# Layer-1 score masks and the guards' schedule moved towards VectorE's queue in a two-layer graph-attention kernel

## The reference

```
adj  = maximum(adj, eye(n))
keys, queries, values = x @ Wks, x @ Wqs, x @ Wvs          # per head
atts = einsum('hqk,hmk->hqm', queries, keys) / key_dim**0.5
atts = atts - 1e16 * (1.0 - adj)
atts = softmax(atts, axis=-1)
out  = einsum('hqm,hmk,hko->qo', atts, values, Wo)
```

## Time and profile before

| what | us |
|---|---|
| median of 3 runs (4674.9 to 4680.1) | 4676.87 |
| the profiled execution, its own time | 4677.4 |
| its span, first to last instruction | 4675.6 |
| TensorE busy, share of the span | 4440.1, 95% |
| VectorE busy | 3542.8, 76% |
| GpSimd busy | 3434.2, 73% |
| ScalarE busy | 3246.9, 69% |
| TensorE granted clock, mean of the span | 0.978 of full speed |

### The profile page before, as it was taken

The page is one execution under the profiler, slowest core; times in us unless marked ns, Lnnn a source line. Parts: engine busy times, 40 slices in busy tenths (PEclk is TensorE's granted clock), DMA queues, the critical chain, the costliest instruction groups (busy, mean ns, idle before and its releaser), DMA issues. The chain is left out here.

```text
span 4675.6 us, 112897 instructions
## 1 busy us (share of the span) xinstructions
PE 4440.1 (95%) x43276; PEld 2137.3 (46%) x43276; DVE 3542.8 (76%) x7470; ACT 3246.9 (69%) x6022; POOL 3434.2 (73%) x2955
## 2 busy tenths in 40 slices
PE   8699999999999978969999999999999999999998
PEld 4222222222222224416556655656655566556555
DVE  5498998988989843367777777777777777777776
ACT  5366666666666633318878878878878788788786
POOL 2476676676776720029989989989989899899897
PEclk9899999999999989969999999999999999999999
DMA  3566776676676533353333433433423334334333
GB/s 143 131 210 196 202 224 201 204 211 208 206 213 184 169 112 112 106 174 86 111 112 92 127 101 90 127 101 99 124 83 111 112 93 130 98 88 127 103 102 102
DMA packets 462941, 646.14 MB, mean 138 GB/s; under 512 B 49536, under 2 KB 271104, under 8 KB 452288
## 3 DMA queue, kind: packets, MB, share of 16 engines
q1 hardware_dynamic: 383968, 522.36, 37.7%
q10 hardware_dynamic: 73856, 100.83, 6.8%
q0 software_dynamic: 4576, 15.73, 1.2%
HBM read 528.38 MB, written 110.38 MB: 137 GB/s over the span
## 5 line engine op out<-in xcount | busy, mean ns | idle before, releaser
L1398 POOL TENSOR_TENSOR d_PL<-d_PF,d_PH 128x512 f16<-128x512 f32 x2048 | 2324.3, 1171 | 296.0 <-ACT d_PH L1448 293.1
L1488 DVE CUSTOM_DVE_ANT_0 d_junk<-d_gd,d_MR 128x512 bf16<-128x512 f32 x2112 | 1441.9, 689 | 500.4 <-issue 465.3
L1444 ACT ACTIVATE d_PF<-d_sc 128x512 f32<-128x512 f32 x2048 | 1283.1, 627 | 518.4 <-DVE d_sc L1577 317.2
L1448 ACT ACTIVATE d_PH<-d_sc 128x512 f16<-128x512 f32 x2048 | 1292.3, 631 | 0.0
L809 DVE SCALAR_TENSOR_TENSOR b_P<-R,u,b_A 128x512 f32<-128x512 f32 x1792 | 1195.3, 738 | 108.8 <-PE b_den L867 58.8
L860 PE MATMUL b_acc<-b_P,V 128*64 128x512 f32 x4096 | 967.7, 608 | 77.8 <-DVE b_P L809 38.3
L1616 PE MATMUL d_gd<-d_KA,d_QA 128*128 128x512 f16 x2112 | 815.6, 387 | 60.6 <-DMA d_KA<-scratch_kl 30.6
L1632 PE MATMUL d_sc<-d_QA,d_KA 128*128 128x512 f16 x2048 | 776.8, 379 | 2.1 <-DVE d_QL L1501 2.1
L1633 PE MATMUL d_sc<-d_QL,d_KB 128*128 128x512 f16 x2048 | 776.3, 379 | 0.0
L1653 PE MATMUL d_acc<-d_V,d_PH 128*128 128x65 f16 x8192 | 638.9, 192 | 2.9 <-ACT d_PH L1448 0.2
L1655 PE MATMUL d_acc<-d_V,d_PH 128*128 128x64 f16 x8192 | 639.9, 193 | 0.0
(11 more groups left out here) (133 smaller groups left out, 4352.7 us busy)
## 6 DMA issues: line engine op xcount, KB each, us to landing
d_V<-scratch_v SPq DMA_DIRECT2D x131, 520.0 KB, 4.6
stage<-in_adjT SPq DMA_DIRECT2D x128, 512.0 KB, 4.5
b_srow<-in_adj ACTq DMA_DIRECT2D x256, 256.0 KB, 5.0
b_rows<-in_adj SPq DMA_DIRECT2D x112, 512.0 KB, 6.6
d_MR<-scratch_mr SPq DMA_DIRECT2D x36, 1024.0 KB, 5.4
d_MT<-scratch_mt SPq DMA_DIRECT2D x35, 1024.0 KB, 6.3
d_KA<-scratch_kh SPq DMA_DIRECT2D x272, 128.0 KB, 3.0
d_KA<-scratch_kl SPq DMA_DIRECT2D x272, 128.0 KB, 3.2
```

The lines of the kernel that those rows point to most:

```text
L1398: eng.tensor_tensor(PL[:, t % H_RING, :], PF[:, t % F_RING, :], PH[:, t % H_RING, :], ALU.subtract).then_inc(s_lowp if by_pool(t) else s_l ...
L1444: nc.scalar.activation(PF[:, t % F_RING, :], sc[(nb * TILES + t) % BANKS][:, :], ACT.Exp, scale=EXP_SCALE)
L1448: nc.scalar.activation(PH[:, t % H_RING, :], sc[(nb * TILES + t) % BANKS][:, :], ACT.Exp, scale=EXP_SCALE).then_inc(s_P, 1)
L1488: nc.vector.tensor_tensor_reduce(out=junk[:, gi % 2, :], in0=gd[gi % 2][:, :], in1=MR[:, s, c * QB:(c + 1) * QB], scale=1.0, scalar=-3.0e3 ...
```

## The change

Three things, all in `layer1_attention`:

1. `masked_by_vector`: before, every fourth tile (`t % 4 == 3`: x = 1 of the odd steps; 64 a block). After, in pair 0 every second tile (x = 1 of every step), in the other pairs `t % 8` in 3, 5, 7 (x = 1 of every step but 0, 4, 8, ..., 28). That is 32 + 3 * 24 = 104 a block. For each tile that changes sides, the matmul L1635 goes and an instruction L1577 comes; ScalarE then waits for VectorE.
2. `guards_of`: still 64 a pair, now from step 1 to step 28, three in the steps 4, 8, 12, 14, 16, 20, 24 and 28, two in the others. ROW_FREE moves from steps 9, 16, 23, 29 to 9, 15, 22, 29 of pair 2.
3. `mask_setup` moves from step 6 of pair 2 to its step 29, and the four `mask_diagonal` from `ROW_FREE + 4` (steps 13, 20 and 27 of pair 2 and step 1 of pair 3) to steps 30 and 31 of pair 2 and 0 and 3 of pair 3.

```diff
-    FIRST_G, LAST_G = 2, 28
+    FIRST_G, LAST_G, EXTRA_G = 1, 28, 14
...
+    def guard_count(mb):
+        if not FIRST_G <= mb <= LAST_G:
+            return 0
+        return 3 if mb % 4 == 0 or mb == EXTRA_G else 2
+
     def guards_of(mb):
-        def upto(step):
-            return GUARDS * min(max(step - FIRST_G + 1, 0), LAST_G - FIRST_G + 1) // (LAST_G - FIRST_G + 1)
-        return range(upto(mb - 1), upto(mb))
+        first = sum(guard_count(k) for k in range(mb))
+        return range(first, first + guard_count(mb))
+
+    assert sum(guard_count(mb) for mb in range(NT)) == GUARDS
...
-    DIAG_STEP, SETUP_STEP = (HP - 2) * NT + 1, (HP - 2) * NT + 6
-    ROW_SET = [free + 4 for free in ROW_FREE]
+    DIAG_STEP, SETUP_STEP = (HP - 2) * NT + 1, (HP - 1) * NT - 3
+    ROW_SET = [(HP - 1) * NT + late for late in (-2, -1, 0, 3)]
...
     def masked_by_vector(t):
-        return t % 4 == 3
+        return t % 2 == 1 if t < PAIR else t % 8 in (3, 5, 7)
```

## The result

The changed kernel takes 4604.16 us (median of 4 runs, 4600.57 to 4608.29) against 4678.42 for the kernel before in the same runs: ratio 0.9845, 95% interval 0.9833 to 0.9857, 74 us faster. I had forecast 4655 with a range of 4610 to 4688: right in sign, wrong in size, outside the range by 6 us. The time lies close to the first rival, "TensorE stays the bound throughout" (4593), but not by that rival's sum alone: the experiments show that more than a third of the gain comes from the guards' schedule, which neither the forecast nor the rival counted.

The account below looks back on a forecast made before the run. The prediction took TensorE as the bound. Per block it saved 8.62 + 1.9 = 10.5 us and lost 7.75, net -2.8, times 8 blocks -22 us: 4677.4 becomes 4655, range 4610 to 4688.

Parts of the forecast that it names:

- TensorE stays the bound throughout: Rival: every loss absorbed, -84 us, 4593; half of the losses absorbed, -53, 4624; chance 0.20 for a time below 4632.
- Item 2: Steps 3 and 4 after a change of pairs: VectorE comes later and normalises later, so guards come 0.55 us late.
- Item 3: mask_setup at step 29 holds VectorE 1.92 us and delays later masks; 1.1 us lost once a block.
- item 4: Masked steps with three guards: VectorE falls 0.5 us behind; 2.4 lost in pair 0, 0.15 in each other pair.
- -84: Sum in us were TensorE to stay as full as now: 69.0 from the masks and 15.2 from mask_setup.
- What the edits take away: The list of savings: 40 matmuls off TensorE, 8.62 us a block, and mask_setup out of the guards, 1.9 a block.
- Item 1: Change of pairs, step 30 to step 2: ScalarE has no gap, TensorE waits; the copy of acc[0] comes 0.35 us later.
- My table: VectorE against TensorE per step, us: masked, two guards 2.09, 2.24; unmasked, three 2.60, 2.68; masked, three 2.96, 2.46.
- VectorE becomes the bound: Rival: a guard behind a mask also pays the 0.25 us gap, masked step 2.34 against 2.24; +45 us, 4722; chance 0.12.
- What is saved is lost again: Rival: the lags of items 1 to 4 are 30% above the estimate, 10.1 us a block; 4674; chance 0.17.

Follow-up runs that it names:

- guards_only: The kernel before with only the new deal of guards (steps 1 to 28, three at multiples of 4 and at 14): 4651.2 us, ratio 0.9943.
- threes_even: The kernel before with guards still on steps 2 to 28, but all ten steps of three on even ones: 4660.5 us, ratio 0.9951.
- The delays: The kernel before with small reductions added on VectorE ahead of normalise's multiply: two (0.65 us) ratio 1.0003, three (0.97 us) ratio 1.0074.
- setup_back: The changed kernel with mask_setup and the mask_diagonals back at their old steps: 4642.1 us, ratio 0.9927 to the kernel before.
- three reductions: The kernel before with three small reductions on VectorE ahead of normalise's multiply, once a pair: 4709.35 us, ratio 1.0074.
- all_x1_g0: The changed kernel with every x = 1 tile masked by VectorE and guards from step 0 to 28, threes at 11, 14, 17, 20, 24, 28: 4584.0 us.

## Why the prediction was wrong

Three terms of the sum failed, all the same way: the guards' schedule was put at nothing and is worth 27 us; the waits of items 2 and 3 took for VectorE's own work what was a wait for GpSimd; and item 4 charged a gap that a late queue doesn't have. By item:

- **What bounds the kernel: right. That 74 us came where -84 stood beside the forecast: in part luck.** TensorE is the bound before and after, a matmul of 0.2155 us leaves in full at the steps where VectorE follows, and mask_setup's stall is real (pair 2: 79.1 to 75.8). But the -84 are masks and mask_setup alone, and of the 74 the guards' schedule brings 27 by itself.
- **A term put at nothing: the guards' schedule.** "What the edits take away" has no line for it, and item 4 makes it a loss of 0.15 a pair, "as today's steps of three masked at 7, 15 and 23 cost nearly as much". guards_only shows -26.7 us, 3.5 a block, of the 6.4 a block that I was off. A step of three that VectorE also masks costs more than one that it doesn't (threes_even), and I weighed only the one that was added, at step 14, against the three that went.
- **The saving was put too high.** Item 1 says that a matmul less at steps 30, 0 and 2 brings nothing, and in pair 1 that is what the steps show; yet the sum saves all 40. That is 9 matmuls, 1.9 us a block too much, which hid part of the other errors.
- **Item 1, change of pairs: right in mechanism, half in size.** The copy is 0.40 later (0.35 forecast; the terms written there give 0.33). TensorE's step 3 is only 0.19 later, since the copy itself took 0.40 instead of 0.59.
- **Item 2, the lag at steps 3 and 4: the wait that failed.** "Only then normalises (1.53, ...)" took a row's duration for VectorE's work. It is 0.7 of work and up to 1.0 of waiting for GpSimd. A queue that comes 0.77 later finds GpSimd nearly done. Of 0.55 us a pair nothing came: step 4 of pair 1 takes 2.68 us before and after. The delays show both sides of it (nothing for 0.65 us, 34 us for 0.97). The rows ahead of the prediction had the sign in them: other VectorE instructions over 512 columns take 0.69, this and L1469 1.6 and 1.7. Beside the earlier trace rows I told the other half, a GpSimd tile of 1.63 us beside L1469, and the rule behind it. The Trainium skill (SBUF - State Buffer, "Who interferes with whom") says that issue order decides which of the two engines blocks. The trace agrees: the multiply came 0.13 us behind GpSimd's start and took 1.6, and the GpSimd instruction behind it 1.6 as well. I had priced it for GpSimd alone and not for the multiply.
- **Item 3, mask_setup at step 29: the same error.** I put 1.92 us between the masks and 1.1 lost. With no subtraction waiting behind the running one L1469 takes 0.68, and the start of pair 3 lost 0.2 more than those of pairs 1 and 2.
- **Item 4, masked steps of three: mis-sized.** I had 2.4 in pair 0. From guards_only to setup_back its steps 3 to 29 lose 1.2 of their masks' 2.8 us, half of it at step 8. My table charges 0.87 for a guard behind a guard. Once VectorE is late, TensorE's result is already there and most of the gap of 0.25 goes: 3108.67 to 3109.39 above is 0.72. A late queue runs faster than one in step. At step 24 of a pair 0 in the changed kernel the first guard starts at 3082.17 and the next step's at 3084.70: 2.53 for a masked step of three against TensorE's 2.46, not 2.96.
- **The rival "VectorE becomes the bound"** rested on the same gap: it had a guard behind a mask pay it too, and those start 0.61 after the mask in the changed kernel. The one called "What is saved is lost again" lies 6 us from masks_only (4668 against 4674), which has the masks without the other two edits.
- **The range** was cut too tight. 4610 is 67 us below the kernel before, four fifths of the way to -84 and not the two thirds that I wrote, but the losses were four guesses that shared one reading, and the sum had no term for the schedule.

## What to carry to other kernels

Before a duration goes into a sum, compare it with the same engine's other instructions of that size: what is longer may be a wait inside the row, and such a wait shrinks when the queue ahead of it grows. A gap of an engine that is in step with another is no cost of the instruction either; it goes when the engine falls behind. An edit that changes no engine's work, such as the schedule here, still needs a term in the sum. And edits can be worth more together: try them together before one is dropped, since the masks alone were worth 7 us. Last, look at the granted clock by stretch when a stall of the bounding engine has grown: it can cost more than its length.

## What the runs showed of the hardware

VectorE's multiply with both inputs in SBUF, and the compare of L1477 from SBUF to SBUF (start and duration together 1.24, its own work 0.28), wait for GpSimd's f32 subtraction of 512 columns until about 1.0 us of its 1.16. The guards and masks, which read one input from PSUM, do not: all 2112 guards take 0.67 to 0.69 us. GpSimd in turn waits for VectorE's, 1.6 instead of 1.16. When the next subtraction is ready, VectorE can lose its turn to it, and more than one. With three reductions, at 1.09 us behind GpSimd's start, 25 of 31 multiplies lost one and 6 none. Three were lost twice in all_x1_g0 (started at 0.94) and once in the profiled execution of the changed kernel (at 0.64). VectorE's row there:

```profile
3644.43 4.42 DVE L1520 TENSOR_TENSOR d_oR<-d_oC,d_rd 128x512 f32<-128x512 f32 x1
```

The four GpSimd instructions it stood behind, none of them lengthened:

```profile
L1404 POOL TENSOR_TENSOR d_PL<-d_PF,d_PH x4: 1167/1171/1178, 3643.8 to 3647.1; 128x512 f16<-128x512 f32 x4
```

TensorE's guard behind them (in brackets: idle before, and for whom):

```profile
3649.60 0.58 PE L1622 MATMUL d_gd<-d_KA,d_QA 128*128 128x512 f16 x1 [3.11 <-DVE d_gm L1494]
```

That pair took 4.2 us more than its like in the other blocks, which is what this execution (4608.29) lies above the median (4604.16). Why it lost three turns there, when others that came at the same point lost none, no run tells.
